# Half-tile causal masks, joined head normalisation, a rebuilt set-up, and the value bias of three layers moved behind the output projection

## The reference

```
for l in 0..3:
    h = layernorm(x)
    q = h @ Wq + bq;  k = ctx @ Wk + bk;  v = ctx @ Wv + bv
    s = q @ k.T / sqrt(8)            # layer 2: causal mask, -inf where key > query
    o = softmax(s) @ v               # layer 3: only the 51 queries of each head that score highest keep their row
    x = x + tanh(g_xattn[l]) * (o @ Wo + bo)
    x = x + tanh(g_ffn[l]) * ffn_l(layernorm(x))   # 0: router and one matrix; 1, 2: mixtures of experts; 3: FP6 blocks
```

## Time and profile before

| | |
|---|---|
| runs of before | 971.24, 969.91, 967.12 us; median 969.91 us |
| the profiled execution | 970.4 us, of which the span from first to last instruction is 968.6 us |
| mean granted TensorE clock | 0.965 of full speed |
| PE busy | 889.0 us (92%) |
| DVE busy | 720.5 us (74%) |
| ACT busy | 631.4 us (65%) |
| POOL busy | 460.4 us (48%) |

### The profile page before, as it was taken

The page is one execution under the profiler, slowest core; times in us unless marked ns, Lnnn a source line. Parts: engine busy times, 40 slices in busy tenths (PEclk is TensorE's granted clock), DMA queues, the critical chain, the costliest instruction groups (busy, mean ns, idle before and its releaser), DMA issues.

```text
span 968.6 us, 22499 instructions
## 1 busy us (share of the span) xinstructions
PE 889.0 (92%) x7921; PEld 609.4 (63%) x7921; DVE 720.5 (74%) x2307; ACT 631.4 (65%) x1441; POOL 460.4 (48%) x559
## 2 busy tenths in 40 slices
PE   4797889999999999999987999999999999999963
PEld 2243347765799987478533465756579987877522
DVE  6897978776653378997999899797644446757897
ACT  2486757766775536797674777767787448686740
POOL 8536644862753134444366266554552524522333
PEclk9599999999999999999997899999999999999977
DMA  6423141221101000002102021020110010010000
GB/s 164 118 63 102 44 132 40 80 62 36 27 22 40 17 1 19 21 24 61 36 21 73 19 73 36 19 52 19 31 41 2 17 34 19 2 35 1 21 2 22
DMA packets 67501, 39.92 MB, mean 41 GB/s; under 512 B 8247, under 2 KB 65360, under 8 KB 67392
## 3 DMA queue, kind: packets, MB, share of 16 engines
q1 hardware_dynamic: 63088, 29.85, 12.1%
q0 software_dynamic: 2208, 6.78, 2.5%
q10 hardware_dynamic: 2096, 1.85, 0.7%
HBM read 11.19 MB, written 1.05 MB: 13 GB/s over the span
## 4 chain that ended last, share of the span: by engine, by line
PE 69%; DVE 16%; POOL 7%; issue 4%; ACT 3%; DMA 0%; SPq 0%; DVEq 0%; ACTq 0%; POOLq 0%
PE banks L984 13%; PE banks L975 13%; PE banks L816 8%; DVE mx L1296 7%; PE banks L944 6%; PE banks L796 5%; PE banks L777 5%; PE banks L763 4%; POOL h L588 3%; PE banks L954 3%; PE banks L756 2%; ACT probs L678 2%; PE banks L913 2%; PE banks L803 2%; POOL rstd L584 1%
## 5 line engine op out<-in xcount | busy, mean ns | idle before, releaser
L1296 DVE TENSOR_REDUCE mx<-banks 128x4 f32<-128x1024 f32 (+1 forms) x240 | 285.1, 1217 | 33.7 <-PE banks L777 24.4
L678 ACT ACTIVATE probs<-banks 128x512 f32<-128x512 f32 (+1 forms) x512 | 259.5, 576 | 71.8 <-PE banks L796 46.9
L731 ACT ACTIVATE probs<-banks,b_sb 128x256 f32<-128x256 f32 x288 | 118.5, 472 | 75.8 <-PE banks L975 74.1
L816 PE MATMUL banks<-probs,v_aug 128*9 128x256 f32 (+1 forms) x2048 | 150.9, 377 | 6.0 <-ACT probs L678 5.2
L584 POOL TENSOR_TENSOR rstd<-veps,mhalf 128x2 f32<-128x2 f32 x64 | 48.0, 750 | 202.4 <-DVE veps L1256 201.9
L984 PE MATMUL banks<-w_sb,probs 128*128 128x128 f32 x1152 | 141.1, 276 | 0.1
L984 PEld LDWEIGHTS banks<-w_sb,probs 128*128 128x128 f32 x1152 | 135.8, 192 | 5.6 <-issue 1.8
L618 POOL TENSOR_TENSOR rn<-ss,mhalf 128x32 f32<-128x32 f32 x16 | 88.1, 5505 | 104.7 <-DVE ss L1097 104.7
L975 PE MATMUL banks<-hT,w_sb 128*128 128x256 f32 x576 | 137.1, 382 | 0.0
L975 PEld LDWEIGHTS banks<-hT,w_sb 128*128 128x128 f32 x576 | 104.5, 190 | 13.5 <-issue 0.6
L796 PE MATMUL banks<-q_st,k_st 64*128 64x256 bf16 (+1 forms) x1024 | 97.7, 274 | 10.1 <-issue 4.1
(11 more groups left out here) (195 smaller groups left out, 1439.4 us busy)
## 6 DMA issues: line engine op xcount, KB each, us to landing
k_st<-k_parts SPq DMA_DIRECT2D x192, 64.0 KB, 2.0
q_st<-q_parts SPq DMA_DIRECT2D x192, 64.0 KB, 2.0
w_sb<-in_w POOLq DMA_DIRECT2D x16, 256.0 KB, 3.8
fc_sb<-in_fc POOLq DMA_DIRECT2D x6, 256.0 KB, 3.5
cT<-in_ctxT SPq DMA_DIRECT2D x8, 128.0 KB, 2.5
x_in<-in_x SPq DMA_DIRECT2D x8, 128.0 KB, 3.9
out_x<-xs SPq DMA_DIRECT2D x8, 128.0 KB, 1.8
q_st<-mT SPq DMA_DIRECT2D x32, 16.0 KB
```

Of the source, the lines that this page charges most:

```text
L678: nc.scalar.activation(probs[s][:, part % UNIT_RING, 2 * a:2 * a + 2, 0:n], b_bank(w, a + 1)[:, 0:2 * n].rearrange("p (j q) -> p j q", j=2 ...
L731: ins = nc.scalar.activation(hid[s][:, part % UNIT_RING, c, :], b_bank(w, half + 1)[:, j * ROWS:(j + 1) * ROWS], ACT.Gelu, bias=b1_sb[:, p ...
L816: ins = nc.tensor.matmul(c_bank(b, l, u // 4)[VW * i:VW * i + VR, g % 2, q0:ROWS], v_aug[s][:, t, 4 * g + i, :], probs[s][:, u % UNIT_RING ...
L1296: nc.vector.tensor_reduce(mx[s][:, r, :, hp0:hp0 + n], banks[:, first:first + 2, :].rearrange("p a (n k) -> p a n k", n=n), AX.X, ALU.max) ...
```

## The change

Five things, besides new tables.

1. **Values.** In layers 0 to 2 the product of context and Wv goes to a second "b" bank, and ACT copies it into `v_aug` without a bias. Layer 3 keeps the DVE addition. Once, in setup part 3, PE multiplies the bias columns of three layers, spread to 128 columns by DVE, by Wo, and DVE adds that, times tanh(g), into `gbo`. The bias columns are loaded by three DMAs of 128 single elements, and Wv and Wo of layers 1 to 3 now belong to the attention loads, so that there are ten DMAs where there were six.
2. **Masks.** The mask product of 128 contracted rows for each bank is replaced by two products of 64 rows: one with the lower or upper half of the unit matrix and the mask as they lie (`mask_b`), one with the halves swapped (`mask_swapped`, made by two DMAs). There are four products where there were two, each with as many columns, and lower and upper half alternate as in the scores.
3. **Heads.** The two banks are neighbours (by the table), and one reciprocal of 128x32 and one product of 128x256 stand where two of each stood; both wait for the second bank.
4. **Start.** ACT loads the first weights, SP loads x first. The banks are cleared by eight PE products with a cleared tile instead of eight DVE memsets. DVE, not POOL, makes h of the first layer for the first four batches, and clears slot 3 too. ACT issues three of the six key and query copies of batches 0 and 1 in layer 0. All ten attention loads stand behind ACT's part of the first query.
5. **Setup.** ACT makes the scaled `bo` rows, the reordered weights and the rank table, which DVE made. ACT and DVE both wait for the attention loads, ACT in setup part 0 and DVE in part 1.

```diff
-PAIRED = True
-DVE_SLOTS = 1
-EARLY_LOADS = 3
+PAIRED = 2
+CLEARED_BY_DVE = (0, 3)
+SPLIT_STREAMS = 2
+EARLY_LOADS = 2
...
-0001103021011332010210203000001110002000110122233112201010000311311000322100020020120201130121131012
+0001332200220011110000003010320113101000011022112321300110010110021023231002030200102300112011212121
...
-        "keys": {"a_full": 1, "a_read": 1, "b_full": 1, "b_read": 1, f"hi_ready{s}": 1, f"k_split{s}": 2, f"k_moved{s}": 16 * TERMS},
+        "keys": {"a_full": int(l == SPARSE), "a_read": int(l == SPARSE), "b_full": 1 + (l < SPARSE), "b_read": 1 + (l < SPARSE), f"hi_ready{s}": 1, f"k_split{s}": 2, f"k_moved{s}": 16 * TERMS},
...
-1023546710324567012345670123445670123045601374526013745201674501267324567201456701245367201436720134
+0123456701234567012345260175623014576230174567230167450123567012356701546237401672340167450267304523
...
-        identb = sb("identb", [P, P], BF16)
-        cqk_b = sb("cqk_b", [P, P], BF16)
-        ckq_b = sb("ckq_b", [P, P], BF16)
+        mask_b = sb("mask_b", [P, 3, P], BF16)
+        mask_swapped = sb("mask_swapped", [P, 3, P], BF16)
+        identb, cqk_b, ckq_b = (mask_b[:, i, :] for i in range(3))
...
         attention_loads = [
             (rows_in, bias_rows[:, R_BO:R_GB].broadcast_to([P, R_GB - R_BO])),
             (wqk_in[:, 1:LAYERS, :, :].rearrange("d l j n -> d l (j n)"), attn_w[:, 1:LAYERS, 0:2, :].rearrange("d l j n -> d l (j n)")),
+            (wvo[:, 1:LAYERS, :, :].rearrange("d l j n -> d l (j n)"), attn_w[:, 1:LAYERS, 2:4, :].rearrange("d l j n -> d l (j n)")),
+            *((bv_col[:, n:n + 1], bias_rows[0, R_BV + n * D:R_BV + (n + 1) * D].rearrange("(d o) -> d o", o=1)) for n in range(SPARSE)),
             (r0_sb[:, :], router0), (cqk, causal_qk), (ckq, causal_kq), (before_f, before_in)]
...
+            def set_up_rows(part):
+
+                if part == 0:
+                    if STEP["keys", 1, 0, 0] > STEP["setup", 0, 0, 0]:
+                        for dst, src in attention_loads[EARLY_LOADS:]:
+                            act.dma_start(dst, src).then_inc(attn_loaded, 16)
+                    act.wait_ge(attn_loaded, 16 * len(attention_loads))
+                    act.wait_ge(gates_done, 1)
+                    for n in range(LAYERS):
+                        nc.scalar.activation(gbo[:, n, :], rows_in[:, n * D:(n + 1) * D], ACT.Copy, scale=tg[:, n:n + 1])
+                    nc.scalar.activation(gbo[:, LAYERS, :], rows_in[:, R_BF3 - R_BO:R_BF3 - R_BO + D], ACT.Copy,
+                                         scale=tg[:, 2 * LAYERS - 1:2 * LAYERS]).then_inc(gbo_scaled, 1)
...
+                    if step == "keys" and l < SPARSE:
+                        act.wait_ge(sems["b_full"], w.at("b_full", 2))
+                        nc.scalar.activation(v_aug[s][:, :, :, 0:HD],
+                                             b_bank(w, 2)[:, 0:RT * D].rearrange("p (t h d) -> p t h d", t=RT, d=HD), ACT.Copy)\
+                            .then_inc(sems["b_read"], 1)
+                    if b < SPLIT_STREAMS and l == 0:
+                        name, terms, st = ("k", K_TERMS, k_st[s]) if step == "keys" else ("q", Q_TERMS, q_st[s])
+                        act.wait_ge(*CLEARED[s])
+                        act.wait_ge(sems[f"hi_ready{s}"], w.at(f"hi_ready{s}", 1))
+                        move_parts(act, terms, 0, st, parts[s], sems[f"{name}_moved{s}"])
+                if step == "query" and (b, l) == (0, 0):
+                    act.wait_ge(gates_loaded, 16 * len(gate_loads))
+                    nc.scalar.activation(tg[:, :], gates[:, :], ACT.Tanh).then_inc(gates_done, 1)
+                    for dst, src in attention_loads[:EARLY_LOADS]:
+                        act.dma_start(dst, src).then_inc(attn_loaded, 16)
+                if (step, b, l) == ("keys", 1, 0) and STEP["keys", 1, 0, 0] < STEP["setup", 0, 0, 0]:
                     for dst, src in attention_loads[EARLY_LOADS:]:
                         act.dma_start(dst, src).then_inc(attn_loaded, 16)
...
+            pe.wait_ge(zeros_ready, 1)
+            for n in range(BANKS):
+                nc.tensor.matmul(banks[:, n, :], q_st[0][:, 0, 0:P], q_st[0][:, 0:2, :].rearrange("p h q -> p (h q)"),
...
-                    for a in range(2):
-                        nc.tensor.matmul(a_bank(w, a + 1).rearrange("p (n k) -> p n k", n=n)[:, :, keys - P:keys], identb[:, :],
-                                         cqk_b[:, :].unsqueeze(1).broadcast_to([P, n, P]), start=False, stop=True)\
-                            .then_inc(sems["a_full"], 1)
+                    for tile in (mask_b, mask_swapped):
+                        for a in range(2):
+                            ins = nc.tensor.matmul(a_bank(w, a + 1).rearrange("p (n k) -> p n k", n=n)[:, :, keys - P:keys],
+                                                   tile[a * HALF:(a + 1) * HALF, 0, :],
+                                                   tile[a * HALF:(a + 1) * HALF, 1, :].unsqueeze(1).broadcast_to([HALF, n, P]),
+                                                   start=False, stop=tile is mask_swapped)
+                            if tile is mask_swapped:
+                                ins.then_inc(sems["a_full"], 1)
...
+                if step == "setup" and b == 0 and part == 3:
+                    pe.wait_ge(bv_spread, 1)
+                    wait_bank("a", 1)
+                    for n in range(SPARSE):
+                        ins = nc.tensor.matmul(a_bank(w, 1)[:, n * D:(n + 1) * D], bv_bc[:, n, :], wvo[:, n, 1, :],
+                                               start=True, stop=True)
+                    ins.then_inc(sems["a_full"], 1)
...
-            for n in range(BANKS):
-                nc.vector.memset(banks[:, n, :], 0.0)
+            clear_queries(nc.vector, 0).then_inc(zeros_ready, 1)
...
+                    for n in range(SPARSE):
+                        spread = nc.vector.tensor_copy(bv_bc[:, n, :], bv_col[:, n:n + 1].broadcast_to([P, P]))
+                    spread.then_inc(bv_spread, 1)
...
+                    dve.wait_ge(gbo_scaled, 1)
+                    dve.wait_ge(sems["a_full"], w.at("a_full", 1))
+                    for n in range(SPARSE):
+                        ins = nc.vector.scalar_tensor_tensor(gbo[:, n, :], a_bank(w, 1)[:, n * D:(n + 1) * D], tg[:, n:n + 1],
+                                                             gbo[:, n, :], ALU.mult, ALU.add)
+                    ins.then_inc(sems["a_read"], 1)
...
-                if step == "keys":
-                    if l == 0 and b < SLOTS:
-                        dve.wait_ge(values_loaded, 16 * len(value_loads))
-                    if l == 1:
-                        dve.wait_ge(late_loaded, 16 * len(late_loads))
+                if step == "keys" and l == SPARSE:
+                    dve.wait_ge(late_loaded, 16 * len(late_loads))
                     dve.wait_ge(sems["a_full"], w.at("a_full", 1))
-                    bv = over_tiles(bv_all[:, l * D:(l + 1) * D], D).rearrange("p t (h d) -> p t h d", d=HD)
+                    bv = over_tiles(bv_row[:, :], D).rearrange("p t (h d) -> p t h d", d=HD)
                     nc.vector.tensor_tensor(v_aug[s][:, :, :, 0:HD],
                                             a_bank(w, 1)[:, 0:RT * D].rearrange("p (t h d) -> p t h d", t=RT, d=HD), bv,
                                             ALU.add).then_inc(sems["a_read"], 1)
...
+                    if (b, l) == (0, 0):
+                        clear_keys(nc.vector, 0, cleared_dve)
+                        clear_queries(nc.vector, 3)
+                        clear_keys(nc.vector, 3, cleared_dve)
+                if step == "norm" and l == 0 and b < SLOTS:
+
+                    dve.wait_ge(sems["rstd_ready"], w.at("rstd_ready", 1))
+                    for r in range(RT):
+                        ins = nc.vector.tensor_scalar(h[s][:, r, :], x_in[s][:, r, :], mv[s][:, r, 0:1],
+                                                      rstd[s][:, r:r + 1], ALU.subtract, ALU.mult)
+                    ins.then_inc(sems[f"h_ready{s}"], 1)
...
-                    pair = [a_bank(w, r + 1).rearrange("p (h v) -> p h v", v=VW) for r in range(RT)]
-                    for r in range(RT):
-                        dve.wait_ge(sems["a_full"], w.at("a_full", r + 1))
-                        end(nc.vector.reciprocal(rden[s][:, r, :], pair[r][:, :, HD]), "shares", b, l, r)
+                    first = w.bank("a", 1)
+                    pair = banks[:, first:first + RT, :].rearrange("p r (h v) -> p r h v", v=VW)
+                    dve.wait_ge(sems["a_full"], w.at("a_full", RT))
+                    end(nc.vector.reciprocal(rden[s][:, :, :], pair[:, :, :, HD]), "shares", b, l)
...
+                    wait_end("shares", b, l)
+                    nc.vector.tensor_tensor(heads_out[s][:, :, :].rearrange("p r (h d) -> p r h d", d=HD),
+                                            pair[:, :, :, 0:HD],
```

(2 more changed lines are left out.)

314 lines of the change are left out of this document (164 added, 150 removed).

## The result

The changed kernel takes 977.66 us (median of five runs, 975.75 to 977.83) against 969.91 for the kernel before. The ratio is 1.0067 with a 95% interval of 1.0045 to 1.0090: slower by 0.67%, some 6.5 us, where 1.4% faster was forecast.

A forecast was written before the change was run, and what follows sets the result against it. PE was taken to bound the two long stretches (62% of the span), DVE most others, loads and first maxima the start. 970.4 - 9.8 (PE) - 6.3 (DVE) + 2 (start) = 956.3, forecast 956 us, range 943 to 968.

The forecast's parts named there:

- PE, -9.8 us: Masks and new order on PE: 98 fewer changes of product shape at 0.10 us each, 9.8 us less.
- here PE's work alone sets the time: Stretches from 150 to 450 and 600 to 900 us: PE, busy 298.9 and 298.6 of 300 us, bounds them.
- what would make it wrong altogether: Order of steps: one that keeps an engine waiting where nothing in the kernel before shows a wait; no size given.
- DVE, -6.3 us: DVE's stretches: values and heads take 8.4 us off DVE, three quarters of it counts, 6.3 us; ends 0 and 8.4.
- The values' share: Value copies moved from DVE to ACT: 13 of 0.416 us fall away where DVE bounds, 5.4 us before three quarters.
- The heads': Paired heads steps on DVE: 0.70 us in place of 0.85, 0.15 less each, 3.0 us together before three quarters.
- the DVE gain goes nowhere: Rival for DVE's stretches: products and ACT's queue pace them, and the start costs its full price; 965 us, chance 0.17.
- Start, +2 us: Start: first scores wait behind bias product and attention loads, first maxima at 25.4 to 28 us; +2 us, ends -4 and +4.5.
- Part of it comes back: Behind the start: DVE's gaps in batch 1 and fewer values recover part of 1.9 to 4.5 us, leaving +2.
- half masks run one after another: Rival for PE's masks: lower and upper half don't run side by side, 28 us more, 984 us; chance 0.06.
- a fixed price for each added mask product: Rival for PE's masks: 224 added products at 0.025 us cost 5.6 us, 962 us; chance 0.04.
- slower for another cause in the order: Rival for the order of steps: some other cause there makes the kernel slower, 976 us or more; chance 0.05.

The follow-up runs named there:

- after_old_order: The changed kernel with unpaired heads, put into the order of steps and banks of the kernel before: 984.37 us, ratio 1.0140 to the kernel before.
- after_old_tail: The changed kernel with its new order up to step 2012 and the old order behind it: 980.98 us, ratio 1.0106 to the kernel before.

## Why the prediction was wrong

**PE, -9.8 us: the step that failed.** "The orders count 785 changes of shape before and 687 after, 98 fewer: 98 x 0.10 = 9.8 us less on PE. 79 of them are the masks', 19 are the new order's." The price is right, and the counts are near: the traces have 80 fewer by the masks on the old order, and 110 fewer in all. What failed is turning them into time. First, "here PE's work alone sets the time": the masks' 7.9 us measured nothing in the old order (1.0001), since in the fullest stretch 41 changes took 4.2 us of scores and masks off PE and 0.4 us off the time. Second, the new order went into the sum by its 19 changes alone. That count holds only with the masks already in (30 by the traces); with whole masks the order has 33 more changes, and it costs 15.9 us. The prediction put every other effect of the order at nothing, though it named it as what would make it wrong altogether.

**DVE, -6.3 us.** The values' share (4.1 us after the factor of three quarters) measured 0.6, at most 2.2. The heads' (2.3 us after it) measured nothing: the 32-element reciprocal takes 0.352 us where 0.26 was taken, and the gap behind it is 0.10, not 0.03, so a step saves nothing of the 0.15. What came through is the lower end of the prediction's range for this term, 0, within the intervals. The rival "the DVE gain goes nowhere" was right on this term.

**Start, +2 us.** The mechanism was forecast as it came: scores behind the bias product, behind the attention loads. The times were too short at three links. ACT's part of the first query ended at 13.5 us, not at 12.5. The ten loads took 5.7 us to their last issue, which at 20.78 lay within the 19 to 21 given, but this last one took 5.1 us to land and not 3.5 to 4, so the loads were in at 25.85 and not by 25. And setup, bias product and additions took 4.2 us and not 3, so the first maxima came at 30.04 where 25.4 to 28 was given. The eight bank-clearing products took 3.6 us where 1.7 stood, and the first keys product starts behind them, at 5.41; what that costs no run shows. "Part of it comes back" is not shown. In after_old_order nothing came back in 940 us. In the changed kernel's own trace the +6.5 is +3.8 at step 406, but in after_old_tail, the same program there, +7.3 is +8.5.

**Masks side by side, no price for added products, ACT copies at 0.39 us, no harm to the exponentials** (ACT waits 60.4 us for scores ahead of them, 67.5 before): right. The rivals "half masks run one after another" and "a fixed price for each added mask product" are refuted: 0.11 us a pair of 256 columns. The Trainium skill's rule of some 60 cycles for each matmul (TensorEngine Tiling (Array Packing), Instruction Overhead) does not show as an addition in these rows; the measurement decides.

**The side.** The outcome, 977.66, lies in the case "slower for another cause in the order", which had 0.05. Sized by the experiments: the new order +15.9, the masks in it -6.4, values and heads with the old start +5.3, the rebuilt start -8.4, sum +6.4. These are steps along one path, each the difference of two ratios, so that they add up to the whole by themselves; on another path (old order first) the same parts have other prices (masks 0, values 0, then +13.6 with the start): order and content count together. What the changed kernel lacks against before has a likely place for about half: 3.0 us go with the loads and the bias product of the start. The rest, 0.36%, has no single place in the splices and stays open.

## What to carry to other kernels

An order written out by numbers is part of the content: price it by running the old content in the new order, before adding up what the new content saves. Engine time saved in a stretch where one engine is busy for 99% is only a bound on the gain: here waits for the other engines, of 0.2 to 0.4 us each, and somewhat slower products elsewhere took all of it. Don't build on a late start being absorbed: in after_old_order 12.7 us were carried to the end in full. And trace the same program twice before reading 3 us, or a stretch's clock, out of one profile: here equal programs differed by up to 5 us, and and by 0.84 against 0.62 in the clock of one stretch of 10 us.

## What the runs showed of the hardware

A change between products of 64 and of 128 rows costs 0.10 us of PE; between 128 rows and column groups it is about 0.09 (a weighing starts 0.32 us behind a mask pair in the kernel before, a turn 0.23 behind one). Half-row masks run side by side at 0.11 us for a pair of 256 columns. With 24 tiles of scores repeated the granted clock was 1.00 from 20 to 30 us, where the traces of before and of the kernels that are the same as it or nearly so there have 0.61 to 0.84, and the time did not change. Three loads of 128 single elements took 2.38 us together to issue on ACT's queue. The first table load on ACT took 1.28 us and stood ahead of the first keys, where the kernel before has it at 1.15 us, ahead of an early tanh:

```profile
6.55 1.28 ACT L675 ACT_TABLE_LOAD   x1 [6.55 <-PE banks L885]
7.85 0.47 ACT L675 ACTIVATE k_parts<-banks,bcol 128x256 bf16<-128x256 f32 x1
```
